# Deeper input buffering, and weight loads moved to the GpSimd queue, in a fused layer-norm / low-rank / int8-FFN kernel

## What is computed

```python
xn  = (u - mean(u)) / sqrt(var(u) + 1e-5)                 # [4096, 2048] on each core
s   = butterfly(xn @ Wbr @ Wbs, A) @ Wcr @ Wcm + Dv * xn  # rank 64, 256 states
w_q = round(Wff / w_scale); w_scale = max|Wff row| / 127  # [2048, 2048]
x_q = round(xn / x_scale);  x_scale = max|xn row| / 127
g   = silu((x_q @ w_q.T) * x_scale * w_scale + bias)
out = u + s * g
```

## Time and profile before

| | us |
|---|---|
| median of 2 runs | 946.31 (934.04 and 958.57) |
| the profiled execution | 931.13 |
| its span, on its slowest core (core 3) | 929.6 |
| spans of the eight cores | 899.8 to 929.6 |
| PE / VectorE / ScalarE / GpSimd busy | 556.8 / 666.5 / 273.8 / 80.4 |

### The profile page before, as it was taken

The page is one execution under the profiler, slowest core; times in us unless marked ns, Lnnn a source line. Parts: engine busy times, 40 slices in busy tenths (PEclk is TensorE's granted clock), DMA queues, the critical chain, the costliest instruction groups (busy, mean ns, idle before and its releaser), DMA issues.

```text
span 929.6 us, 7756 instructions; the slowest of 8 cores (899.8 to 929.6 us)
## 1 busy us (share of the span) xinstructions
PE 556.8 (60%) x2368; PEld 239.3 (26%) x2368; DVE 666.5 (72%) x754; ACT 273.8 (29%) x239; POOL 80.4 (9%) x152
## 2 busy tenths in 40 slices
PE   0022111000020989885989698697979879999990
PEld 0011010000000434332333243233324334444440
DVE  0887466743443798984999699789989897677762
ACT  0000001442534224342343351544345332011100
POOL 1000000110110011000100001010001110000000
PEclk9999999999995989998889899899989999999996
DMA  7459999968765655798679969957976974843531
GB/s 145 166 175 233 160 222 163 223 130 138 145 130 148 102 185 176 201 240 147 212 178 248 164 182 190 251 164 212 240 222 177 271 229 172 237 181 134 206 136 45
DMA packets 134955, 169.23 MB, mean 182 GB/s; under 512 B 110210, under 2 KB 110274, under 8 KB 124674
## 3 DMA queue, kind: packets, MB, share of 16 engines
q0 software_dynamic: 16272, 75.78, 29.4%
q10 hardware_dynamic: 14194, 67.77, 23.5%
q1 hardware_dynamic: 104448, 25.19, 22.4%
HBM read 101.86 MB, written 58.72 MB: 173 GB/s over the span
## 4 chain that ended last, share of the span: by engine, by line
DVE 27%; DMA 26%; PE 24%; issue 10%; ACT 8%; ACTq 2%; POOL 1%; DVEq 1%; POOLq 0%
PE ffnps L605 21%; DMA vh<-v 18%; DMA o<-Wff 4%; DMA wdh<-y 4%; DVE y L472 3%; ACT v L223 3%; DVE stats L345 3%; DVE y L511 3%; DVE s L495 3%; DVE stats L343 3%; ACT v L235 2%; DVE stats L400 2%; PE z3ps L576 2%; ACT v L227 2%; DVE y L413 2%
## 5 line engine op out<-in xcount | busy, mean ns | idle before, releaser
L605 PE MATMUL ffnps<-wT,slabB 128*128 128x512 f16 x1024 | 236.6, 393 | 44.9 <-DVE y L511 44.9
L605 PE MATMUL ffnps<-wT,slabA 128*128 128x512 f16 x1024 | 238.2, 395 | 31.4 <-DVE y L511 31.4
L605 PEld LDWEIGHTS ffnps<-wT,slabB 128*128 128x128 f16 x1024 | 101.6, 101 | 179.3 <-issue 70.3
L605 PEld LDWEIGHTS ffnps<-wT,slabA 128*128 128x128 f16 x1024 | 102.0, 101 | 167.2 <-issue 59.2
L249 ACT ACTIVATE y<-y 128x2048 f16<-128x2048 f16 x32 | 61.2, 1912 | 251.5 <-DVE y L511 246.6
L223 ACT ACTIVATE v<-u 128x2048 f16<-128x2048 f16 x32 | 61.2, 1912 | 224.6 <-DMA vh<-v 211.4
L511 DVE SCALAR_TENSOR_TENSOR y<-ffnps,stats,brep 128x1024 f16<-128x1024 f32 x64 | 79.9, 1278 | 37.3 <-PE ffnps L605 37.1
L343 DVE TENSOR_REDUCE stats<-u 128x1 f32<-128x2048 f16 x32 | 73.0, 2281 | 39.6 <-DMA u<-u 39.4
L576 PE MATMUL z3ps<-slabA,wbr 128*64 128x512 f16 x64 | 16.0, 407 | 118.6 <-DMA slabA<-vh 118.6
L495 DVE TENSOR_TENSOR s<-z3ps,s 128x2048 f16<-128x2048 f32 x32 | 73.3, 2292 | 14.5 <-PE z3ps L588 11.2
L472 DVE SCALAR_TENSOR_TENSOR y<-s,stats,y 128x2048 f16<-128x2048 f16 x32 | 75.2, 2351 | 5.4 <-ACT y L249 2.2
(11 more groups left out here) (70 smaller groups left out, 285.8 us busy)
## 6 DMA issues: line engine op xcount, KB each, us to landing
o<-u ACTq DMA_DIRECT2D x32, 1024.0 KB, 6.3
out<-o POOLq DMA_DIRECT2D x32, 1024.0 KB, 4.7
u<-u POOLq DMA_DIRECT2D x32, 512.0 KB, 9.4
o<-Wff ACTq DMA_DIRECT2D x16, 1024.0 KB, 9.6
vh<-v POOLq DMA_DIRECT2D x32, 512.0 KB, 10.3
vr<-vh ACTq DMA_DIRECT2D x32, 512.0 KB, 9.2
wdh<-y POOLq DMA_DIRECT2D x16, 512.0 KB, 12.2
wT<-wdh SPq DMA_TRANSPOSE x64, 7.6
```

The costliest lines, as they stand in the source:

```text
L605: PE.sig(reg, tensor.matmul(ffnps[:, og * 512:(og + 1) * 512], slab[(c // 4) % 2][:, dch, (c % 4) * 128:(c % 4 + 1) * 128], wT[:, dch, og ...
```

## The change

- u16 has four slots instead of two (with four semaphores), and the unused results of `front_a` go to a new tile junk: `front_a` no longer waits for `vh:cc-2`. `front_b` does instead, or, for the first two tiles, for the last weight pieces in v16.
- Wff is loaded by GpSimd's queue, cast to float16, into four slots (s16 and v16, which the stage doesn't use otherwise): four pieces behind the first four tiles of u, then piece oc+4 behind the store of piece oc. ScalarE's loads and their waits go, and its evictions of that stage run without interruption.
- The order of the front: in the prologue `front_b(k-3)` follows `front_a(k)`, and six tiles of v are stored ahead of the loop instead of eight. In the loop `front_b` and `vstore` take tile c+6 instead of c+8, and `z2e` for the next slab stands ahead of `front_a` instead of behind it.

The wait in vector L490 for the weight pieces in s16, and the order of `urload` and `vrload`, follow from these. The diff, cut to its core:

```diff
-        u16 = sb("u16", [128, 2, D], F16)
+        u16 = sb("u16", [128, 4, D], F16)
+        junk = sb("junk", [128, D], F16)
...
-            for oc in range(2):
-                W[oc % 2].sig(reg, scalar.dma_start(
-                    out=o32[:, oc % 2, :], in_=wff_h[oc * 128:(oc + 1) * 128, :]),
-                    f"ld:w:{oc}")
...
             def front_a(cc):
                 w(f"ld:u16:{cc}")
-                if cc >= 2:
-                    w(f"vh:{cc - 2}")
...
-                    out=v16[:, cc % 2, :], in_=u16[:, cc % 2, :],
+                    out=junk[:], in_=u16[:, cc % 4, :],
                     func=ACT.Identity, accum_out=st(SUMU)), f"sc:id:{cc}")
...
             def front_b(cc):
                 w(f"dv:stats2:{cc}")
+                if cc >= 2:
+                    w(f"vh:{cc - 2}")
+                else:
+                    w(f"dv:vws:{14 + cc}")
...
-            drain_ev(1)
-            for oc in range(DCH):
-                quant(oc)
-                if oc >= 2:
-                    drain_ev(3)
             drain_ev(99)
             urload(0)
             urload(1)
             nf = min(LAG, C)
-            front_a(0)
-            for k in range(1, nf):
+            nb3 = max(nf - 3, min(4, C))
+            for k in range(min(3, nf)):
                 front_a(k)
-                front_b(k - 1)
+            for k in range(3, nf):
+                front_a(k)
+                front_b(k - 3)
+            for k in range(max(nf - 3, 0), nb3):
+                front_b(k)
             vrload(0)
-            vrload(1)
             for c in range(C):
                 if c >= 1:
                     silu(c - 1)
+                if c % 4 == 3 and c + 1 < C:
+                    z2e((c + 1) // 4)
                 if c + LAG < C:
                     front_a(c + LAG)
-                kb = min(LAG, C) - 1 + c
-                if kb < C:
-                    front_b(kb)
-                if c == 0:
+                if c + nb3 < C:
+                    front_b(c + nb3)
+                if c == max(0, 3 - nb3):
                     z2e(0)
-                if c % 4 == 3 and c + 1 < C:
-                    z2e((c + 1) // 4)
...
+            wslot = [s16[:, 0, :], s16[:, 1, :], v16[:, 0, :], v16[:, 1, :]]
             for oc in range(DCH):
...
-                                                 in0=o32[:, oc % 2, :],
+                                                 in0=wslot[oc % 4],
                                                  scalar1=so(WINV), scalar2=None,
                                                  op0=ALU.mult), f"dv:vws:{oc}")
...
             def uload(cc):
-                if cc >= 2:
-                    w(f"sc:v:{cc - 2}")
-                    w(f"dv:umin:{cc - 2}")
+                if cc >= 4:
+                    w(f"sc:v:{cc - 4}")
+                    w(f"dv:umin:{cc - 4}")
...
-            uload(0)
-            uload(1)
+            for cc in range(min(4, C)):
+                uload(cc)
+            for oc in range(4):
+                wload(oc)
             for oc in range(DCH):
                 w(f"dv:wdeq:{oc}")
                 WH[oc % 2].sig(reg, gpsimd.dma_start(
                     out=wdh[oc * 128:(oc + 1) * 128, :], in_=y16[:, oc % 2, :]),
                     f"wh:{oc}")
+                if oc + 4 < DCH:
+                    wload(oc + 4)
+            nf = min(LAG, C)
+            nb3 = max(nf - 3, min(4, C))
             for k in range(min(LAG + 1, C)):
                 rstd(k)
-                if k + 2 < min(LAG + 1, C):
-                    uload(k + 2)
-                if k < min(LAG, C) - 1:
+                if 4 <= k + 4 <= LAG and k + 4 < C:
+                    uload(k + 4)
+                if k < min(nb3, C):
                     vstore(k)
             for c in range(C):
...
                 if c + LAG + 1 < C:
                     uload(c + LAG + 1)
-                kb = min(LAG, C) - 1 + c
-                if kb < C:
-                    vstore(kb)
+                if c + nb3 < C:
+                    vstore(c + nb3)
```

More of the change, by code:

```diff
@@ L125, in build @@
         GST = Track("GST", sem("GST"), 16)
-        UL = [Track(f"UL{i}", sem(f"UL{i}"), 16) for i in range(2)]
+        UL = [Track(f"UL{i}", sem(f"UL{i}"), 16) for i in range(4)]
         UR = [Track(f"UR{i}", sem(f"UR{i}"), 16) for i in range(2)]
         VR = [Track(f"VR{i}", sem(f"VR{i}"), 16) for i in range(2)]
-        W = [Track(f"W{i}", sem(f"W{i}"), 16) for i in range(2)]
+        W = [Track(f"W{i}", sem(f"W{i}"), 16) for i in range(4)]
         WH = [Track(f"WH{i}", sem(f"WH{i}"), 16) for i in range(2)]
@@ L200, in urload @@
                     w(f"st:{cc - 2}")
-                else:
-                    w(f"dv:vws:{14 + cc}")
                 UR[cc % 2].sig(reg, scalar.dma_start(
@@ L233, in front_b @@
                 w(f"dv:stats2:{cc}")
+                if cc >= 2:
+                    w(f"vh:{cc - 2}")
+                else:
+                    w(f"dv:vws:{14 + cc}")
                 scalar.wait_ge(SC.sem, SC.n)
                 SC.sig(reg, scalar.activation(
-                    out=v16[:, cc % 2, :], in_=u16[:, cc % 2, :],
+                    out=v16[:, cc % 2, :], in_=u16[:, cc % 4, :],
                     func=ACT.Identity, scale=st(A2), bias=st(B2P)), f"sc:v:{cc}")
@@ L294, in _ @@
                     silu(c - 1)
+                if c % 4 == 3 and c + 1 < C:
+                    z2e((c + 1) // 4)
                 if c + LAG < C:
                     front_a(c + LAG)
-                kb = min(LAG, C) - 1 + c
-                if kb < C:
-                    front_b(kb)
-                if c == 0:
+                if c + nb3 < C:
+                    front_b(c + nb3)
+                if c == max(0, 3 - nb3):
                     z2e(0)
-                if c % 4 == 3 and c + 1 < C:
-                    z2e((c + 1) // 4)
                 if c >= 1 and c + 1 < C:
                     urload(c + 1)
-                if c + 2 < C:
-                    vrload(c + 2)
+                vof = min(nb3, 2)
+                if c == 0:
+                    for k in range(1, min(vof + 1, C)):
+                        vrload(k)
+                elif c + vof < C:
+                    vrload(c + vof)
             silu(C - 1)
@@ L342, in dfront @@
                 w(f"ld:u16:{cc}")
-                DV.sig(reg, vector.reduce_max(out=st(UMAX), in_=u16[:, cc % 2, :],
+                DV.sig(reg, vector.reduce_max(out=st(UMAX), in_=u16[:, cc % 4, :],
                                               axis=AX.X), f"dv:umax:{cc}")
                 DV.sig(reg, vector.tensor_reduce(out=st(UMIN),
-                                                 in_=u16[:, cc % 2, :],
+                                                 in_=u16[:, cc % 4, :],
                                                  axis=AX.X, op=ALU.min),
@@ L399, in _ @@
                 w(f"ld:w:{oc}")
-                DV.sig(reg, vector.reduce_max(out=so(WMAX), in_=o32[:, oc % 2, :],
+                DV.sig(reg, vector.reduce_max(out=so(WMAX), in_=wslot[oc % 4],
                                               axis=AX.X, apply_absolute_value=True),
@@ L488, in _ @@
                 w("sc:drepe")
+                if c <= 1:
+                    w(f"dv:vws:{12 + c}")
                 selfw()
@@ L627, in uload @@
             def uload(cc):
-                if cc >= 2:
-                    w(f"sc:v:{cc - 2}")
-                    w(f"dv:umin:{cc - 2}")
-                UL[cc % 2].sig(reg, gpsimd.dma_start(
-                    out=u16[:, cc % 2, :], in_=u_h[cc * 128:(cc + 1) * 128, :]),
+                if cc >= 4:
+                    w(f"sc:v:{cc - 4}")
+                    w(f"dv:umin:{cc - 4}")
+                UL[cc % 4].sig(reg, gpsimd.dma_start(
+                    out=u16[:, cc % 4, :], in_=u_h[cc * 128:(cc + 1) * 128, :]),
                     f"ld:u16:{cc}")
@@ L653, in outst, with wload @@
                     in_=o32[:, cc % 2, :]), f"st:{cc}")
-            uload(0)
-            uload(1)
+            wsl = [s16[:, 0, :], s16[:, 1, :], v16[:, 0, :], v16[:, 1, :]]
+            def wload(oc):
+                W[oc % 4].sig(reg, gpsimd.dma_start(
+                    out=wsl[oc % 4], in_=wff_h[oc * 128:(oc + 1) * 128, :]),
+                    f"ld:w:{oc}")
+            for cc in range(min(4, C)):
+                uload(cc)
+            for oc in range(4):
+                wload(oc)
             for oc in range(DCH):
```

## The result

The changed kernel takes 1017.5 us (median of 11 executions, 999.8 to 1033.1) against 943.5 for the kernel before, run beside it: a ratio of 1.078 with an interval of 1.067 to 1.088, slower. The prediction was 993.9, within 938 to 1040. The profiled execution took 1012.8, its span on the slowest core (core 7) is 1011.3. Executions of one kernel spread by several per cent here; ratios compare undisturbed ones, and where fewer than two of these are left only a median stands.

What follows compares the result with a forecast made beforehand. The prediction took ScalarE's round trips to bound the prologue and VectorE the loop, PE from iteration 28. From 931.1 us profiled, 27.9 gained at the start and 90.7 lost to slabs gave 993.9, range 938 to 1040.

Steps and rivals of the forecast that it cites:

- The slabs: Main loop: v stored two iterations later leaves each slab's transposes a 16.1 us window, so PE waits; +90.7 us.
- 62.5 + G: Main loop: predicted us from slab to slab, one iteration, store, landing, transposes and the way to the next iteration.
- 102.8 + 2G: End of the loop: predicted us for slabs 6 and 7 together, against 139.0 before.
- G: Time a slab's 16 transposes take, last landing included: 34 us for slabs 1 to 5, 27 for 6 and 7.
- my cycle: Main loop, slab to slab: 18.6 iteration, 15.4 to the store, 11.6 landing, slab time, 16.9 to the next iteration.
- The start: Prologue: PE's first z3 at 272.3 us, 27.9 earlier than before, with the weight stage still ending at 165.
- my rival with the stores caught behind loads: Weight stage: store landings of 16, stage end at 180, first z3 at 287, total 1009 us; chance 0.09.
- SyncE's chain: Prologue: four weight groups until 242.51, then slab 0's transposes on SyncE's queue, put first z3 at 272.3 us.
- the front's round trips: Prologue: load, three ScalarE passes, load, 14.2 to 16.1 us each, five times; first z3 at 263 to 272.
- The rule: SyncE's weight groups: transposes beside two queues get half the turns instead of a third; first two groups 80 us.
- the rival with faster weight groups: SyncE's queue: groups 1 and 2 near the last two's pace, start at 263, total 985 us; chance 0.10.
- the loop's loss of 90.7: Main loop: us added by waits for slabs, seven slab times (224) minus 133.3.

Runs made afterwards that it cites:

- run 1: Changed kernel with eight tiles of v stored ahead of the loop, front_b and vstore taking tile c+8 again: 934.5 us, too widely spread for a ratio.
- run 2: Changed kernel with nb3 = 7, so front_b and vstore take tile c+7, halfway back: 992.8 us.
- run 5: Changed kernel with nb3 = 8 and z2e back behind front_a and front_b: 921.8 us, ratio 0.975 to the kernel before.
- run 6: Changed kernel with nb3 = 8, z2e back behind the fronts and weight loads back on ScalarE's queue: 917.6 us, ratio 0.979 to the kernel before.
- run 3: Changed kernel with z2e put back behind front_a and front_b: 1025.5 us, ratio 1.083 to the kernel before.
- run 8: run 5 with the stores of wdh moved from GpSimd's to ScalarE's queue: 922.3 us, ratio 0.981 to the kernel before.
- run 9: run 5 with the prologue's order of the kernel before, a load running two tiles ahead: 926.8 us, ratio 0.984 to the kernel before.
- run 10: run 9 with slab 0 transposed ahead of the last weight group on SyncE's queue: 908.3 us, ratio 0.964 to the kernel before.
- run 7: Changed kernel with the store of v ahead of rstd and uload on GpSimd's queue, lag unchanged: 1001.3 us, ratio 1.067 to the kernel before.

## Why the prediction was right, and by how much it was off

**The slabs.** Right as mechanism and nearly as size. Link by link above; the stretches of the profiled core were 94.1, 389.3 and 162.2 where 62.5 + G once, four times that, and 102.8 + 2G gave 96.5, 386.0 and 156.8 with my G of 34 and 27. G was 33.5 over slabs 1 to 5 of the eight cores. That it came so close is in part luck: my sum had 29.0 for the 16 issues and 5.4 for the last landing, and they took 31.5 and 1.8. (In its reading of slab 2, nine issues lie ahead of the stalled one, not ten; nine, that one and six more are the 16 of the sum.) Runs 1, 2, 5 and 6 show that the lag of `front_b` and `vstore` is what costs: undone alone it takes the median core from 987 to 886. (In run 2, the slab took 45, not 30 to 38; the window of the slab shown was 36.4, near the 35 expected.)

**The order on ScalarE.** I charged 4.2 us a slab for `front_a` behind `z2e`, and that link is there. But run 3 shortens it by more than 4 and the time stays: while a slab is late, the held-back front also keeps GpSimd's next load and store off the transposes. The two terms of my cycle, G and this link, are not independent. With the slab on time the order costs some 1.7 a slab (runs 6, 8 and 9 against run 1).

**The start.** First z3 at 285.9 on the profiled core against 272.3, the largest miss (+13.6): its weight stage ended at 176.7, not 165, which lay near my rival with the stores caught behind loads (180, start 287). The number fits that rival, its reason doesn't: run 8. The median core has 268.1, close to the forecast. SyncE's chain is confirmed by runs 9 and 10, the front's round trips as second path are not.

**The rule.** The Trainium skill, "DMA: Bandwidth & Descriptors", section "Queues, rings and completion order", has a DMA engine take turns, packet by packet, between the queues with work. From this I had worked out 80 for the first two weight groups with one queue fewer. On the profiled cores they took 196.03 - 67.88 = 128.2 (119.6 before), the last two 57.9 (57.3); the medians over eight cores are 106.5 (110.4 before) and 58.7 (57.7). The trace does not follow that use of the rule, and the rival with faster weight groups is out.

**The sum.** +13.6 from the start, -2.4, +3.3 and +5.4 from the three stretches, -1.0 behind iteration 28: 18.9, the distance from 993.9 to 1012.8. I also took core 3 of the kernel before, whose loop (333.0 for iterations 4 to 20) was the slowest of eight with a median of 317.3; so the loop's loss of 90.7 was put too small, and on the median core it is 103.

## What to carry to other kernels

A product that is stored later in a reordered pipeline can make another consumer late; it was the lag that cost here, not the deeper ring of u16, which runs 5 and 6 keep. So count for every consumer of the delayed product, here the slab transposes, the iterations between issue and need, and compare them with the longest service time, not the shortest. A transfer's time taken from a stretch in which everything waits for it is too small for a version in which it is to be hidden (33 against 41 to 45 us here). And an edit that shortens a link behind a shared resource has to be read in the whole cycle: runs 3 and 7 shortened theirs and gave it back.

## What I had not expected of the hardware

Moving 16 MB of weight reads from one queue to another, halving the bytes that they write and deepening their buffer from two to four left the end of the weight stage where it was (157 to 163 us, and 158.5 with the stores moved too). The same stage ended between 153 and 177 us on the eight cores of one execution. And one slab of 16 transposes took 21 to 25 us to issue in a quiet stretch, 54 us, twice, on the slowest core of run 9, and 90.6 us on the slowest core of run 5. Such a slab marks the cores that fall behind: in run 5 the three with an issue span over 60 for slab 5 need 330 to 370 for iterations 4 to 20, the other five 312 to 319. Why a core meets one is open.
